# First-stage chunk loads and residual cuts moved from SyncE and VectorE to GpSimd, two score tasks moved among the residues

## What is computed

```python
h = _layernorm(x) * (1 + ca) + sa
q, k, v = split(h @ W_attn + b_attn)                  # 16 heads of 8
att = q @ k.T / sqrt(8) + alibi_causal_mask
y = softmax(att) @ v                                  # 2048 x 2048 a head
x = x + ga * (y @ W_proj + b_proj)
h = _layernorm(x) * (1 + cb) + sb
x = x + gb * top2_experts(h)                          # silu between w1 and w2
```

## Time and profile before

| | us |
|---|---|
| median of 3 runs | 585.2 |
| the profiled execution | 584.42 |
| its span, first to last instruction | 582.6 |
| mean granted TensorE clock | 0.955 |
| TensorE matmul busy | 495.7 (85%) |
| VectorE busy | 456.4 (78%) |
| ScalarE busy | 403.3 (69%) |
| GpSimd busy | 176.2 (30%) |

### The profile page before, as it was taken

How to read it: one execution, slowest core, us unless ns; L and a number is a source line. 1 busy time by engine, 2 the same in 40 slices (tenths; PEclk the granted TensorE clock), 3 DMA queues, 4 the chain that set the end, 5 groups by cost and what they waited for, 6 DMA issues and landing times.

```text
span 582.6 us, 15494 instructions
## 1 busy us (share of the span) xinstructions
PE 495.7 (85%) x5876; PEld 266.1 (46%) x5876; DVE 456.4 (78%) x775; ACT 403.3 (69%) x778; POOL 176.2 (30%) x291
## 2 busy tenths in 40 slices
PE   4756777889999999999999998998988997999960
PEld 2422233343243343243343333334434987999960
DVE  3689999989989998988998998986688744653442
ACT  4922456669878888888888888787788464555520
POOL 3410000010022120410214001057075681870884
PEclk9975899999999999999999999999899997999995
DMA  6593121000012530222300000100221212333332
GB/s 156 198 292 74 30 56 29 1 3 4 11 29 60 169 131 2 92 74 44 78 10 4 2 2 4 30 9 6 88 78 57 78 60 75 104 102 92 106 87 72
DMA packets 38263, 37.86 MB, mean 65 GB/s; under 512 B 7088, under 2 KB 33904, under 8 KB 37560
## 3 DMA queue, kind: packets, MB, share of 16 engines
q1 hardware_dynamic: 35808, 32.26, 20.0%
q0 software_dynamic: 2048, 4.20, 2.4%
q10 hardware_dynamic: 336, 0.42, 0.2%
HBM read 20.05 MB, written 16.61 MB: 63 GB/s over the span
## 4 chain that ended last, share of the span: by engine, by line
PE 51%; ACT 8%; POOL 8%; DVE 6%; issue 4%; DMA 1%; ACTq 0%; POOLq 0%; DVEq 0%
PE pv L744 18%; PE b L777 13%; ACT probs L1295 6%; PE b L716 6%; PE b L851 4%; PE b L868 4%; POOL raw L1470 4%; DVE part L1012 3%; PE b L691 3%; POOL pause L1442 2%; POOL slot_scratch L1449 1%; ACT raw L1265 1%; PE b L646 1%; PE b L842 1%; PE b L663 1%
## 5 line engine op out<-in xcount | busy, mean ns | idle before, releaser
L1295 ACT ACTIVATE probs<-b 128x512 f32<-128x512 f32 (+1 forms) x576 | 298.6, 571 | 77.2 <-PE b L691 34.3
L1012 DVE TENSOR_REDUCE part<-b 128x2 f32<-128x1024 f32 (+2 forms) x320 | 327.4, 1060 | 25.2 <-PE b L691 11.7
L744 PE MATMUL pv<-probs,v_cur 128*32 128x256 f32 (+1 forms) x2432 | 175.3, 370 | 0.3 <-ACT probs L1295 0.2
L777 PE MATMUL b<-aug 55*128 55x512 bf16 (+3 forms) x640 | 113.2, 352 | 24.8 <-ACT probs L1295 20.6
L716 PE MATMUL b<-aug 52*128 52x512 bf16 (+3 forms) x640 | 115.8, 361 | 20.1 <-DVE part L1012 17.2
L777 PEld LDWEIGHTS b<-aug 55*128 55x128 bf16 x640 | 36.9, 93 | 135.7 <-ACT probs L1295 129.8
L744 PEld LDWEIGHTS pv<-probs,v_cur 128*32 128x32 f32 x2432 | 49.9, 108 | 66.5 <-issue 38.9
L851 PE MATMUL b<-hTt,inverse 128*128 128x128 f32 x424 | 58.1, 281 | 1.3 <-ACT hTt L1316 1.1
L868 PE MATMUL b<-w2T_sb,hst 128*128 x424 | 57.1, 279 | 1.2 <-ACT hst L1322 0.8
L851 PEld LDWEIGHTS b<-hTt,inverse 128*128 128x128 f32 x424 | 53.2, 197 | 1.9 <-issue 1.3
L868 PEld LDWEIGHTS b<-w2T_sb,hst 128*128 128x128 f32 x424 | 52.5, 195 | 1.8 <-issue 1.6
(11 more groups left out here) (150 smaller groups left out, 379.0 us busy)
## 6 DMA issues: line engine op xcount, KB each, us to landing
xt<-slot_scratch SPq DMA_DIRECT2D x53, 64.0 KB, 1.9
y_scratch<-aug SPq DMA_DIRECT2D x53, 64.0 KB
slot_scratch<-slots SPq DMA_DIRECT2D x3, 1024.0 KB, 8.6
aug<-q_scratch SPq DMA_DIRECT2D x6, 384.0 KB
aug<-k_scratch SPq DMA_DIRECT2D x6, 384.0 KB
w2T_sb<-in_w2T SPq DMA_DIRECT2D x1, 2048.0 KB, 7.6
aug<-in_w1T SPq DMA_DIRECT2D x8, 256.0 KB
q_scratch<-pieces SPq DMA_DIRECT2D x4, 384.0 KB, 2.8
```

What stands on the lines that cost most here:

```text
L744: return mm(pv[32 * hh:32 * hh + 32, c0:c1], v_cur[:, kb, hh, :], probs[:, step_ % 2, hh, at_:at_ + c1 - c0], start=(kb == 0 and c0 == 0), ...
L777: done.append(mm(pair[half][:, at_:at_ + w], k_aug[g % 2][n, b, kb * P:kb * P + P], q_aug[g % 2][n, b, (j + 1) * CW - w:(j + 1) * CW], sta ...
L1012: ins = nc.vector.tensor_reduce(dst, b1[:, slot:slot + 2, at_:at_ + w], AX.X, ALU.max)
L1295: nc.scalar.activation(probs[:, p % 2, hh, 0:w], b2[:, (n2 - 1) % RING2, 0:w], ACT.Exp).then_inc(exp_done, 1)
```

## The change

Five things are altered.

- **Banks.** Queries and keys go to `b2[0]` and `b2[1]`, turned tokens to `b2[2]`, values to `pv`. All of `b1` but the small products in `b1[3]` is left to the scores.
- **Third pieces.** Of chunk 0 VectorE still makes piece 2. Of chunks 1 to 3 GpSimd makes it (`last_pieces`, two subtractions of 128x512 a chunk).
- **Loads.** The four `load_stack` DMAs of each chunk are issued by GpSimd (`load_chunk`), behind a wait for `piece_out[c]`. SyncE keeps the stores alone.
- **Two tasks early.** TensorE issues tasks 0 and 1 between the query and key products of chunk 3 and its value products; VectorE reduces them ahead of the two `res` subtractions of chunk 3.
- **Memsets.** The two memsets of `v_cur` stand at the start of GpSimd's list.

```diff
+EARLY_TASKS = 2
@@ SyncE
-            for c in range(NC_ + 1):
-                if c < NC_:
-                    sp.wait_ge(piece_s, 2 * (c + 1))
+            for c in range(NC_):
+                sp.wait_ge(piece_s, 2 * (c + 1))
...
-                if c:
-                    sp.wait_ge(piece_out[c - 1], 6 * 16)
-                    load_stack(sp, 0, 0, c - 1, c, aug0_in[c - 1])
@@ TensorE
+            first_at, first_tasks = [0], [0]
             for c in range(NC_):
...
-                    mm(b1[:, n, :], wqkv[:, n * C:(n + 1) * C], hT[:, c * CW:(c + 1) * CW], start=True, stop=True).then_inc(qk_ps, 1)
+                    mm(b2[:, n, :], wqkv[:, n * C:(n + 1) * C], hT[:, c * CW:(c + 1) * CW], start=True, stop=True).then_inc(qk_ps, 1)
                 if c + 1 < NC_:
                     turn_early(c + 1)
...
+                else:
+                    maxima_scores(0, True, first_at, first_tasks, EARLY_TASKS)
+                early_values(c)
...
                             pass1(TSTART[u + 1] + SETTLE0)
+                            if first:
+                                pe.wait_ge(q32_s, 2 * NC_)
+                                pe.wait_ge(v_s, NC_)
                             turn(u)
@@ VectorE
             for c in range(NC_):
+                if c == NC_ - 1:
+                    maxima(EARLY_TASKS, first_tasks, first_at)
                 for n in range(2):
                     dve.wait_ge(q32_s, 2 * c + n + 1)
+                    if c:
+                        dve.wait_ge(piece_s, 2 * (c - 1) + n + 1)
+                    nc.vector.tensor_tensor(res[:, n, :], q32[:, n, :], cut_of(c, n, 0), ALU.subtract).then_inc(res_s, 1)
+                if c == 0:
+                    for n in range(2):
+                        dve.wait_ge(piece2_s, n + 1)
+                        nc.vector.tensor_tensor(cut_of(c, n, 2), res[:, n, :], cut_of(c, n, 1), ALU.subtract).then_inc(piece_s, 1)
+                biased_values(c)
@@ ScalarE
-                    if c:
-                        act.wait_ge(piece_s, 2 * (c - 1) + n + 1)
                     if c >= 2 and n == 0:
                         act.wait_ge(piece_out[c - 2], 6 * 16)
@@ GpSimd
             own.inc(nc.gpsimd.memset(neg_half[:, :], -0.5))
+            own.inc(nc.gpsimd.memset(v_cur[:, :, :, :], 0.0))
+            own.wait()
+            own.inc(nc.gpsimd.memset(v_cur[:, :, :, 3 * D:4 * D], 1.0))
             deviation(0, True)
...
+            def last_pieces(c):
+
+                pool.wait_ge(piece_s, 2 * c)
+                for n in range(2):
+                    pool.wait_ge(piece2_s, 2 * c + n + 1)
+                    nc.gpsimd.tensor_tensor(cut_of(c, n, 2), res[:, n, :], cut_of(c, n, 1), ALU.subtract).then_inc(piece_s, 1)
+
+            def load_chunk(c):
+
+                pool.wait_ge(piece_out[c], 6 * 16)
+                load_stack(pool, 0, 0, c, c + 1, aug0_in[c])
+
+            for c in range(1, NC_):
+                last_pieces(c)
+                load_chunk(c - 1)
+            load_chunk(NC_ - 1)
             pool.wait_ge(v_s, NC_)
```

More of the change, by code:

```diff
@@ L400, in load_stack, with cut_of @@
                     e.dma_start(aug[buf][rows_, :, t0:t1], src[g, half, :, :, t0:t1]).then_inc(done, 16)
+        def cut_of(c, n, piece):
+            return pieces[:, c % 2, n, piece, :]
         def load_alibi(e, g, buf, done):
@@ L604, in turn_early, with early_values @@
                 pe.wait_ge(xn_s, c + 1)
-                if c >= 2:
-                    pe.wait_ge(hT_s, c - 1)
-                turn_tokens(xn, c, b2[:, c % 2, :], xT_ps)
+                if c:
+                    pe.wait_ge(hT_s, c)
+                turn_tokens(xn, c, b2[:, 2, :], xT_ps)
+            def early_values(c):
+                if c:
+                    pe.wait_ge(v_s, c)
+                for i in range(TPC):
+                    t = (TPC * c + i) * P
+                    last = mm(pv[:, i * C:(i + 1) * C], hT[:, t:t + P], wqkv[:, 2 * C:3 * C], start=True, stop=True)
+                last.then_inc(v_ps, 1)
@@ new lines, in mask_out, with maxima_scores @@
+            def mask_out(pair, at_, table, cols):
+                for h, (c0, c1) in enumerate(cols):
+                    for half in range(2):
+                        k = slice(HALF * half, HALF * half + HALF)
+                        ins = mm(pair[half][:, at_ + c0:at_ + c1], identh[k, h, :], table[k, h, c0:c1], start=False, stop=True, skip_group_check=True)
+                return ins
+            def maxima_scores(g, first, at, n_task, upto):
+                while at[0] < upto:
+                    k = at[0]
+                    j, c, rs, b = TASKS[k % NTASK]
+                    buf = (g + k // NTASK) % 2
+                    if first and k < NTASK and k == TSTART[j]:
+                        pe.wait_ge(aug0_in[j], 4 * 16)
+                    if first and k == 0:
+                        pe.wait_ge(const_in[0], 6 * 16)
+                        pe.wait_ge(mask_in, 6 * 16)
+                        pe.wait_ge(masks_s, 2)
+                    if k == NTASK:
+                        take(pe, aug_in, (4 if first else 8) * 16)
+                        if first:
+                            pe.wait_ge(const_in[1], 6 * 16)
+                    n_task[0] += 1
+                    pe.wait_ge(s1_free, n_task[0])
+                    pair = [b1[:, 2 * (k % SLOTS) + half, :] for half in range(2)]
+                    at_ = 0
+                    for r in rs:
+                        w = (r + 1) * P if c == j else CW
+                        for half in range(2):
+                            n = slice(HALF * half, HALF * half + ROWS1)
+                            t = j * CW + r * P
+                            ins = mm(pair[half][:, at_:at_ + w], q_aug[buf][n, b, t:t + P], k_aug[buf][n, b, c * CW:c * CW + w], start=True, stop=True)
+                        if c == j:
+                            ins = mask_out(pair, at_ + r * P, maskQ, ((0, P), (HALF, P)))
+                        at_ += w
+                    ins.then_inc(s1_ready, 1)
+                    at[0] += 1
@@ L682, in group @@
             def group(g, first, last):
[L683 to L692, removed]
-                def pass1(upto):
[L695 to L721, removed]
+                n_task = first_tasks if first else [0]
+                at = first_at if first else [LEAD]
+                def pass1(upto):
+                    maxima_scores(g, first, at, n_task, upto)
                 def turn(u):
@@ L950, in gates, with maxima @@
                 nc.vector.scalar_tensor_tensor(gate[:, :, :], gsgn[:, :, :], -1.0, gabs[:, :, :], ALU.add, ALU.mult).then_inc(gate_s, 1)
+            def maxima(upto, n_task, at):
+                while at[0] < upto:
+                    k = at[0] % NTASK
+                    j, c, rs, b = TASKS[k]
+                    n_task[0] += 1
+                    dve.wait_ge(s1_ready, n_task[0])
+                    slot, at_ = 2 * (k % SLOTS), 0
+                    for r in rs:
+                        w = (r + 1) * P if c == j else CW
+                        dst = part[:, j % 2, :, c].rearrange("p (r s b) -> p r s b", s=2, b=PAIRS)[:, r, :, b]
+                        ins = nc.vector.tensor_reduce(dst, b1[:, slot:slot + 2, at_:at_ + w], AX.X, ALU.max)
+                        at_ += w
+                    ins.then_inc(s1_free, 1)
+                    at[0] += 1
+                    if k + 1 == TSTART[j + 1]:
+                        mine.inc(nc.vector.memset(tick[:, 0:1], 0.0))
+                        mine.wait()
+                        nc.vector.tensor_reduce(nmax[:, j % 2, :, :].rearrange("p r h -> p (r h)"), part[:, j % 2, :, 0:j + 1], AX.X, ALU.max,
+                                                negate=True).then_inc(nmax_s, 1)
@@ L953, in _ @@
+            mine = Own(dve, dve_g)
+            first_at, first_tasks = [0], [0]
+            dve.sem_inc(s1_free, 1)
             for c in range(NC_):
+                if c == NC_ - 1:
+                    maxima(EARLY_TASKS, first_tasks, first_at)
                 for n in range(2):
                     dve.wait_ge(q32_s, 2 * c + n + 1)
[L956 to L964, removed]
+                    if c:
+                        dve.wait_ge(piece_s, 2 * (c - 1) + n + 1)
+                    nc.vector.tensor_tensor(res[:, n, :], q32[:, n, :], cut_of(c, n, 0), ALU.subtract).then_inc(res_s, 1)
@@ L986, in add_sums @@
                 nc.vector.tensor_tensor(unit_y(j), unit_y(j), raw_y(G - 1, j), ALU.add).then_inc(y3_s, 1)
-            mine = Own(dve, dve_g)
             def group(g, first, last):
-                n_task, at = 0, 0 if first else LEAD
+                n_task = first_tasks if first else [0]
+                at = first_at if first else [LEAD]
                 for p in range(-1, NSTEP + 1):
@@ L1002, in group @@
                         nc.vector.reciprocal(last_part(q), last_part(q)).then_inc(last_s, 1)
[L1003 to L1022, removed]
+                    maxima(upto, n_task, at)
```

(15 more changed lines are left out.)

31 lines of the change are left out of this document (11 added, 20 removed).

## The result

| | before | changed |
|---|---|---|
| median, us | 585.58 (584.65 to 586.39, 4 runs) | 594.18 (593.78 to 594.49, 4 runs) |
| ratio | | 1.0151, 95% interval 1.0136 to 1.0165 |
| span of the profiled execution | 582.6 | 592.7 |

The change costs 8.6 us by the medians. GpSimd's timeline of the changed kernel, 20 to 68 us, shows where (start, duration, engine, line, what; idle before in brackets); it answers to the earlier trace rows.

A forecast was written before the change was run, and what follows sets the result against it. The prediction took ScalarE and the stores, then VectorE's reductions, as bounds, with GpSimd's cut holding three engines. Issues near 1 us moved the cut from 43.32 to 52.4: 585.2 + 9.1 = 594.3 us, range 589.5 to 600.

The forecast's parts named there:

- the gate: GpSimd's cut of block 0's maxima, which TensorE, VectorE and ScalarE wait for; forecast to restart them 9.1 us later.
- The cut's end: End of GpSimd's cut of block 0's maxima, within the first 60 us: forecast 52.4 against 43.32 before.
- rival (a): GpSimd's DMA issues are cheap, 0.45 us each; chunk 3 bound by ScalarE; shift 4.5, total 589.7; chance 0.2.
- (b): GpSimd's DMA issues are dear, 1.45 us each; its cut ends at 57.8; shift 14.5, total 599.7; chance 0.17.
- step 5: ScalarE starts chunk 3 at 32.6, 1.8 us later; GpSimd, free at 36.6, subtracts for that chunk until 39.3.
- step 4: GpSimd's loads of chunk 1 wait for that chunk's stores until 32.6 and are issued until 36.6.
- (c): VectorE's lighter load ahead of the restart reaches the end: 584.2, at best 581.9; chance 0.04.
- (d): Work after 60 us that waits for something keeping its time takes up the shift: 585 to 589; chance 0.04.
- VectorE's microsecond: VectorE's `nmax` for block 0 was forecast at about 41, a microsecond earlier than before.
- One for one to the end: After the cut all engines restart 9.1 us later in the same order, and nothing absorbs the shift.
- The rule on issuers: DMAs of all issuers share 16 engines, so issuing loads from GpSimd saves issue time only; transfers gain nothing.
- The rule on the port: VectorE's residues, holding the shared port pair, could hold GpSimd's loads of chunk 0 up to 1.4 us: 595.7.

The follow-up runs named there:

- e1_cut_first: Changed kernel with GpSimd cutting block 0's maxima before it issues chunk 3's loads and copies the values: 586.59 us, ratio to before 1.0014.
- e2_hold_14: Kernel before with fourteen 128x512 memsets on GpSimd between the arrival of block 0's maxima and their cut: 593.15 us, ratio 1.0131.
- e11_stores_alone: Changed kernel with GpSimd's loads of chunk 2 behind the wait for chunk 3's stores: 595.7 us in the one execution looked at.
- neither hold: Kernel before with fourteen or seven memsets on GpSimd ahead of the cut of block 0's maxima: 593.15 us and 589.93 us.
- e6_pieces_alone: Kernel before with third pieces of chunks 1 to 3 on GpSimd and the two memsets at its list's start: 586.13 us, ratio 1.0014.
- e7_loads_back: Changed kernel with all loads back on SyncE in the order of before, third pieces still on GpSimd: 585.46 us, ratio 1.0006.
- e5_tasks_alone: Kernel before with the change's banks, memsets and two early tasks; loads stay on SyncE, third pieces on VectorE: 586.13 us, ratio 1.0009.
- the filler: The e9_rows_sooner version with one 128x128 float32 matmul on TensorE behind each of tasks 4 to 15: 586.77 us, ratio 1.0019.
- e9_rows_sooner: Reworked change: SyncE loads behind each chunk's stores, six early tasks, cut before chunk 3's third pieces, block 0's rows before chunk 2's loads: 582.33 us.

## Why the prediction was right, and where it was not

The mechanism was right. The total to a tenth of a us is luck: the gate's shift was forecast 0.8 too large, two terms in it offset each other, and the medians (8.6 us apart) lie between that shift, 8.26, and the profiled pair's 10.1. The median before itself moved from 585.2 to 585.58 with its fourth run.

- **The gate: right.** GpSimd's cut behind three copies, behind four issues, behind the wait for chunk 3's stores, is in the trace as forecast, and opening it (`e1_cut_first`) or closing it in the kernel before (`e2_hold_14`) moves the time each way.
- **The cut's end: 52.4 forecast, 51.58 measured.** Two terms were mis-sized and offset each other. An issue took GpSimd 0.57 us (the very first 0.85), nearer to SyncE's than to the indirect DMAs' 1.02, from which I took 1.0: 0.4 too much, sixteen times, though the waits for stores hid all but loads 3, 1.7 us. The stores from first issue to complete took 8.2 (25.91 to 34.09) and 8.1 us where I had 7.0: a whole microsecond each, because I took half of 1.3 for a contention that is 1.3 to 1.8 us. By rival (a) as I had summed it, with cheap issues, the cut would have ended at 47.8. The issues were nearly as cheap as that; it was the stores that kept the cut late.
- **Slips in the sum.** Rival (a) leaves the contention out (stores of 6.4 us flat) and (b) takes all 1.3 of it, where the forecast takes half; with the forecast's half, (a) would end at about 49.0. A delay of 1.4 us at loads 0 would have reached step 5 as 0.9, since step 4 waits 0.5 for the stores. Four reductions of eight by columns are 1.8 us, not 1.9 (measured 1.95). The chances of (c) and (d) add up to 0.04 faster and 0.01 same, not 0.05 and 0.02.
- **VectorE's microsecond: wrong.** I had `nmax` at about 41; it starts at 41.90. Step 5 failed by its start: ScalarE's chunk 3 at 34.09, not 32.6, by the same 8.2 us of stores.
- **One for one to the end: right by the medians, 8.6 for 8.26; not in the profiled pair,** where the distance grew to 10.67 while the clock was low. By the span, `nmp` to the end is 1.8 us longer than before, over the microsecond that I had named as a sign of being wrong. The step that failed is the sentence that all engines go on in the same order and nothing changes behind the gate: it left TensorE's clock out.
- **The rule on issuers: borne out.** `e11_stores_alone` shows the sharing, 1.8 us, which the trace before could not. The Trainium skill, "DMA: Bandwidth & Descriptors", section "Issuing engines are not separate DMA queues", says that DMAs of all issuers interleave on the same 16 engines; this trace agrees. **The rule on the port: read too widely.** GpSimd's issues at 26.69 and 27.84 took 0.60 and 0.57 us beside residues on VectorE (26.69 to 27.38, 27.85 to 28.54), others 0.57 alone, and the 1.4 us did not come. The Trainium skill, "SBUF — State Buffer", section "Who interferes with whom", itself says that `tensor_tensor`, which the residues are, has no mode that takes both ports; the trace agrees.
- **Rivals (c) and (d)** did not come about: GpSimd was not free when `nmax` came, and neither hold found slack in the attention.

Open: what decides how long TensorE stays at the lower level. From block 1's maxima to block 2's, the kernel before and the three on its banks (both holds, `e6_pieces_alone`) took 25.7 us, with 4.8 to 5.0 us of it at the lower level. All nine kernels with the new banks and early tasks took 27.5 to 28.4 us, with 13.2 to 14.9 at the lower level. So the growth of 1.8 to 2.7 us comes with these edits and the order on TensorE that goes with them, and goes with the clock, and not with the length of the stall: `e1_cut_first` and `e7_loads_back` have it without a stall, `e2_hold_14` has the stall without it. Nor does it go with where the loads are issued: `e5_tasks_alone` and `e7_loads_back` issue them on SyncE in the old order and have it too. Which of them brings it, no run tells. Each is one profiled execution, and the medians of `e5_tasks_alone` and `e7_loads_back` do not show the loss. I did not settle it.

## What to carry to other kernels

When work moves to a queue that has time, look for the latest thing in that queue that others wait for, and count every wait that now stands ahead of it: here an engine 30% busy held up three for 8.3 us. A wait on a DMA's completion belongs behind whatever is needed sooner, and rows of a hand-written order want the same look on every queue, as the same fault in SyncE's list showed. Two mis-sized terms can give a right total; the steps have to be compared one by one. And where loads start beside stores, as here, look at what waits for each: the loads' new place made the stores longer, and ScalarE stood behind the stores.

## What I had not expected of the hardware

- A plain DMA of 96 KB (48 rows of two 1 KB runs) issued by GpSimd held it for 0.57 us, against 1.0 for an indirect one of 128 rows.
- Four such loads, issued 0.6 to 0.8 us behind the first of six stores, made the stores 1.3 to 1.8 us longer: 7.6 to 8.1 in three kernels against 6.3.
- TensorE was busy for 10.00 of 10 us at the granted clock 0.50 with the filler, and stayed at that level until about 69 us.
- GpSimd's cast and subtraction of 128x16 took 0.50 and 0.53 us beside VectorE's residues in `e9_rows_sooner`, 0.21 each alone.
